# A graph network on one core: the matrix fill split over the engines, and softmax carries applied by masks

## The reference

```python
x = _layernorm(x + _L0_gnn_ref(x, ...), axis=-1)               # attention, 4 heads
x = _layernorm(x + _L1_gnn_ref(x, ...), axis=-1)               # relational
x = _layernorm(x + _L2_gnn_ref(x, edge_weight, src, dst, 3), axis=-1)   # row = src, col = dst
x = _layernorm(x + _L3_gnn_ref(x, edge_index, ...), axis=-1)   # three attention layers, 8 heads

# L2
for _ in range(num_layers):
    msgs = w * X[col]
    X = jax.ops.segment_sum(msgs, row, num_segments=n)
# L0 and L3, per head
m = jax.ops.segment_max(scores, dst, num_segments=N)
e = jnp.exp(scores - m[dst])
denom = jax.ops.segment_sum(e, dst, num_segments=N)
```

## Time and profile before

| | us |
|---|---|
| three runs | 9757.88, 9770.26, 9777.77 |
| median | 9770.26 |
| the profiled execution | 9781.8 |
| its span, first to last instruction | 9780.3 |
| first and last start of the fill's copy on POOL | 3052.9, 4142.0 |
| forward scan of g0 begins, subtraction of g0 begins | 5681.53, 5751.08 |

### The profile page before, as it was taken

One profiled execution on the slowest core, in us unless ns is written; L12 is line 12 of the kernel. 1 busy time (PEld: TensorE's weight loads), 2 busy tenths in 40 slices (PEclk: granted clock), 3 DMA queues, 4 the chain that ended last, 5 costly groups with the idle time before them and its releaser, 6 DMA issues. The chain is left out here.

```text
span 9780.3 us, 183226 instructions
## 1 busy us (share of the span) xinstructions
PE 7267.8 (74%) x30867; PEld 5489.8 (56%) x30868; DVE 6308.2 (64%) x11370; ACT 908.7 (9%) x3742; POOL 4750.5 (49%) x5670
## 2 busy tenths in 40 slices
PE   1899979899997777756666639866663986666388
PEld 1899969788884334313444427644442774444266
DVE  1333356688865777701777867767786776778777
ACT  0222211100010000001000002200000220000012
POOL 0777610477644888800777710077771006777200
PEclk9999999899988999965888969788886987888798
DMA  9444445455531333384777756367775636777564
GB/s 43 113 119 121 118 139 187 118 154 154 151 107 59 108 108 108 114 318 176 187 189 190 196 134 170 105 179 190 192 195 138 169 114 168 188 190 196 143 167 122
DMA packets 1717750, 1476.66 MB, mean 151 GB/s; under 512 B 951333, under 2 KB 1311774, under 8 KB 1717140
## 3 DMA queue, kind: packets, MB, share of 16 engines
q1 hardware_dynamic: 1437876, 949.34, 36.4%
q0 software_dynamic: 163424, 409.43, 16.3%
q10 hardware_dynamic: 116352, 116.73, 3.5%
HBM read 1110.02 MB, written 364.81 MB: 151 GB/s over the span
## 5 line engine op out<-in xcount | busy, mean ns | idle before, releaser
L620 POOL DMA_INDIRECT gx<-table_g,gi x2352 | 2227.4, 947 | 798.9 <-issue 637.0
L859 PE MATMUL ps<-rows,oh 128*128 x5280 | 1722.8, 466 | 1072.6 <-POOLq L597 643.9
L859 PEld LDWEIGHTS ps<-rows,oh 128*128 128x128 f32 x5280 | 1114.3, 227 | 1653.2 <-POOLq L597 844.7
L1196 PE MATMUL ps<-work,oh 128*128 128x273 f32 (+1 forms) x7040 | 1661.2, 405 | 296.7 <-DVE work L1150 261.5
L1196 PEld LDWEIGHTS ps<-work,oh 128*128 128x128 f32 x7040 | 1359.1, 227 | 597.7 <-issue 230.0
L593 POOL COPY gi<-src_i 128x16 int32 (+1 forms) x250 | 51.3, 205 | 2321.9 <-ACTq L694 1670.3
L1150 DVE TENSOR_TENSOR work<-rows,xl 128x1024 f32<-128x1024 f32 (+1 forms) x880 | 872.6, 992 | 471.4 <-PE ps L1196 270.8
L736 DVE TENSOR_TENSOR work<-gx,ps 128x768 f32<-128x768 f32 x660 | 629.8, 954 | 687.3 <-PE ps L861 603.4
L1657 POOL TENSOR_SCALAR oh<-gx,lin 128x196 f32<-128x196 f32 x1176 | 906.2, 785 | 81.7 <-POOL lin L1653 81.2
L1382 PE MATMUL ps<-work,oh 128*128 128x272 f32 x3520 | 862.3, 398 | 45.8 <-issue 31.4
L620 POOL DMA_INDIRECT gx<-table_r,gi x784 | 742.8, 947 | 310.0 <-issue 196.4
(11 more groups left out here) (291 smaller groups left out, 7806.1 us busy)
## 6 DMA issues: line engine op xcount, KB each, us to landing
oh<-hot_d SPq DMA_DIRECT2D x880, 256.0 KB, 2.7
oh<-hotT_d SPq DMA_DIRECT2D x660, 256.0 KB, 3.0
big<-dense_d SPq DMA_DIRECT2D x96, 784.0 KB
dense_d<-big SPq DMA_DIRECT2D x588, 98.0 KB
dense_d<-big ACTq DMA_DIRECT2D x588, 98.0 KB, 1.7
hotT_d<-ohT SPq DMA_DIRECT2D x220, 256.0 KB
hot_d<-oh ACTq DMA_DIRECT2D x220, 256.0 KB, 2.0
ohT<-hotT_d SPq DMA_DIRECT2D x220, 256.0 KB
```

Source lines behind the costliest of these rows:

```text
L620: pool.indirect_dma_start(m.gx[:, u, k, 0:w], None, table, bass.IndirectOffsetOnAxis(m.gi[:, odd, u * K + k:u * K + k + 1].bitcast(U32), 0 ...
L859: ins = nc.tensor.matmul(to, turned, rows, start=True, stop=not adds)
L1196: ins = nc.tensor.matmul(sums(u), m.oh[:, u, k, :], rhs(u % 2)[:, k, :], start=(k == 0), stop=(k == K - 1))
```

## The change

In the fill:

- `places` (0 or 1) and `spots` (times the weight) become two steps. VectorE makes places for two visits in one instruction, with the node numbers read from a PSUM bank, one turn ahead of their use. ScalarE multiplies each by its weight with a Copy activation whose scale is a column of `v_w`.
- POOL makes the high one-hots of visits 0 to 2 of a turn, VectorE that of visit 3 (`last_high`), between its sums.
- `spots`, `his` and `sums` are rings of eight, `places` holds two turns, the PSUM banks remain four; `sums` moves from `m.big` to `m.work`. The loops cover two turns in a pass.
- SP stores visits 0 to 2 and loads their home rows together; ScalarE stores visit 3 two turns late, after the scalings of the turn.
- The filler has 256 columns, not 512. The spill rows are eight, not four.

In the softmax, VectorE makes for each direction, before it waits for the scores, a mask by one scan over the cuts: 0 from a partition's beginning (or end) up to the first cut, -1e30 or less behind it. The backward scans follow the forward scans at once, one carry round serves both directions, and the carry is applied with the mask by an elementwise `max(mask + carry, value)` in place of a second scan.

The diff, cut to its core:

```diff
@@ softmax_parts
+            low = m.work[:, 1, 0:1]
+            step(nc.vector.memset(low, -BIG))
+            for n_way, (way, cuts) in enumerate(zip(ways, (m.new_seg, m.end_seg))):
+                step(nc.vector.tensor_tensor_scan(ends[n_way][:, way], cuts[:, way], low.to_broadcast([P, RUN]),
+                                                  0.0, ALU.add, ALU.max))
+                edge = RUN - 1 if not n_way else 0
+                step(nc.vector.tensor_copy(flags[n_way], ends[n_way][:, edge:edge + 1].to_broadcast([P, heads])))
             dve.wait_ge(s("in"), 16)
...
-                step(nc.vector.tensor_reduce(m.c8[:, 3, 0:1], cuts[:, :], AX.X, ALU.min))
...
                 for h in range(heads):
-                    ins = nc.vector.tensor_tensor_scan(by_head[1][:, h, way], cuts[:, way], by_head[1][:, h, way],
-                                                       carry[:, h:h + 1], ALU.add, ALU.max)
+                    ins = nc.vector.scalar_tensor_tensor(out=by_head[1][:, h, :], in0=ends[n_way],
+                                                         scalar=carries[n_way][:, h:h + 1], in1=by_head[1][:, h, :],
+                                                         op0=ALU.add, op1=ALU.max)
@@ dense_fill, VectorE
+            def place(i, half, c):
+                if not c:
+                    need(dve, s("spots"), (i - 1) * RING)
+                at, wide = c * RING // 2, RING // 2
+                nc.vector.tensor_tensor(
+                    places[:, half, c * wide * P:(c + 1) * wide * P].rearrange("p (n q) -> p n q", n=wide),
+                    node_no.unsqueeze(1).to_broadcast([P, wide, P]),
+                    m.v_key[:, bass.ds(i * RING + at, wide)].unsqueeze(2).to_broadcast([P, wide, P]),
+                    ALU.is_equal).then_inc(s("places"), 1)
+            def last_high(i, odd):
+                nc.vector.tensor_scalar(his[:, odd * RING + last, :], m.hi_no[:, :],
+                                        m.v_hi[:, bass.ds(i * RING + last, 1)], None,
+                                        ALU.is_equal).then_inc(s("last_high"), 1)
-                nc.vector.tensor_scalar(spots[:, u, :], m.iota_row[:, :], m.v_key[:, bass.ds(v, 1)],
-                                        m.v_w[:, bass.ds(v, 1)], ALU.is_equal, ALU.mult).then_inc(s("hot"), 1)
+            def turn(i, odd, more=True):
+                add(i, odd, 0)
+                if more:
+                    place(i + 1, 1 - odd, 0)
+                add(i, odd, 1)
+                if more:
+                    place(i + 1, 1 - odd, 1)
+                add(i, odd, 2)
+                if more:
+                    last_high(i + 1, 1 - odd)
+                add(i, odd, 3)
@@ dense_fill, ScalarE
+            def scale(i, odd):
+                act.wait_ge(s("places"), (i + 1) * 2)
+                act.sem_inc(s("turn_act"), 1)
+                for u in range(RING):
+                    v = i * RING + u
+                    need(act, s("made"), v - 2 * RING + 1)
+                    act.sem_inc(s("spot_act"), 1)
+                    nc.scalar.activation(spots[:, odd * RING + u, :], places[:, odd, u * P:(u + 1) * P], ACT.Copy,
+                                         scale=m.v_w[:, bass.ds(v, 1)]).then_inc(s("spots"), 1)
+            with act.Fori(3, turns - 1, 2) as i:
+                scale(i, 1)
+                store(i - 2, 1)
+                scale(i + 1, 0)
+                store(i - 1, 0)
@@ dense_fill, PE
-                nc.tensor.matmul(m.ps[:, RING + u, :], m.ident_b[:, :], filler, start=True, stop=True)
+                nc.tensor.matmul(m.ps[:, 4 + 2 * (u % 2), 0:2 * P], m.ident_b[:, :], filler, start=True, stop=True)
```

More of the change, by code:

```diff
@@ L1605, in dense_fill, with in_turns @@
 def dense_fill(nc, m):
[L1607 to L1615, removed]
+    places = m.ohT
+    spots = m.work[:, 0, 0:2 * RING * P].rearrange("p (n q) -> p n q", n=2 * RING)
+    his = m.one_hots[:, 0:2 * RING * HIS].rearrange("p (n h) -> p n h", n=2 * RING)
+    sums = m.work[:, 1, 0:2 * RING * HIS].rearrange("p (n h) -> p n h", n=2 * RING)
+    filler = m.iota_b[:, :].unsqueeze(1).to_broadcast([P, K, P])[:, 0:2, :]
+    node_no = m.ps[:, 5, 0:P]
+    stored_rows = m.dense_d.rearrange("(w p) h -> w p h", p=P)
+    turns, last = VISITS // RING, RING - 1
+    def in_turns(eng, turn):
+        for i in range(2):
+            turn(i, i)
+        with eng.Fori(2, turns - 1, 2) as i:
+            turn(i, 0)
+            turn(i + 1, 1)
     with ExitStack() as ctx:
@@ new lines, in _ @@
+            nc.vector.memset(sums[:, 2 * RING - 1, :], 0.0)
+            nc.vector.tensor_copy(node_no, m.iota_row[:, :]).then_inc(s("numbers_set"), 1)
+            dve.wait_ge(s("numbers_set"), 1)
+            for c in range(2):
+                place(0, 0, c)
+            last_high(0, 0)
+            for i in range(2):
+                turn(i, i)
+            with dve.Fori(2, turns - 2, 2) as i:
+                turn(i, 0)
+                turn(i + 1, 1)
+            turn(turns - 2, 0)
+            turn(turns - 1, 1, False)
@@ L1647, in _ @@
             numbers = m.lin[:, 0, 0:RING]
[L1649 to L1658, removed]
@@ L1686, in _, with turn @@
+            for v in range(2 * RING):
+                body(v // RING, v % RING, v // RING)
+            with pe.Fori(2, turns, 2) as i:
+                for odd in range(2):
+                    for u in range(RING):
+                        body(i + odd, u, odd)
         @block.sync
         def _(sp):
-            store(sp, (0, 2))
-        @block.scalar
-        def _(act):
-            store(act, (1, 3))
+            def turn(i, odd):
+                homes = nc.values_load_multi_w_load_instructions(
+                    m.v_home[0:1, bass.ds(i * RING, last)], engines=(mybir.EngineType.SP,),
+                    min_val=0, max_val=NWIN + 2 * RING - 1)[1]
+                for u in range(last):
+                    slot = odd * RING + u
+                    sp.wait_ge(s("summed"), i * RING + u + 1)
+                    sp.sem_inc(s("turn_sp"), 1)
+                    sp.dma_start(stored_rows[bass.ds(homes[u], 1)].rearrange("a p h -> (a p) h"), sums[:, slot, :]
+                                 ).then_inc(s(f"stored{slot}"), 16)
@@ L1695, in dense_layers @@
+            in_turns(sp, turn)
+            for odd in range(2):
+                for u in range(last):
+                    sp.wait_ge(s(f"stored{odd * RING + u}"), 8 * turns)
 def dense_layers(nc, m):
```

122 lines of the change are left out of this document (74 added, 48 removed).

## The result

| | before | after |
|---|---|---|
| runs | 9757.88, 9770.26, 9777.77 | 9870.77, 9873.32, 9876.95 |
| median, us | 9770.26 | 9873.32 |
| span of the profiled execution, us | 9780.3 | 9871.6 |
| turn of the fill, us | 3.717 | 4.096 |

The ratio is 1.0102, with the interval 1.0085 to 1.0119: the change makes the kernel **slower by 1.0%**. The forecast was 9527 us, faster by 2.5%. It was wrong in size and in sign, and its range did not hold the time. The table's turn is taken from GpSimd's copies before and from SyncE's loads after. GpSimd, which runs up to two turns ahead of PE, ends the fill early, so its copies after would give 4.045; SyncE's loads before give 3.72.

A forecast was written before the change was run, and what follows sets the result against it. Pool was taken to bound the fill, with a chain through ScalarE nearly tied, at 2.98 us a turn. From 9781.8 us, minus 216 (fill), 27 (softmax) and 11.5 (profiled run to median), came 9527 us, range 9475 to 9635.

The forecast's parts named there:

- SP's term: In the fill, SP issuing three stores and loading three homes takes 1.5 to 2.6 us a turn.
- Pool at 2.90 to 2.95 us: In the fill, Pool's turn with three one-hots, the copy and two gaps takes 2.90 to 2.95 us.
- VectorE's sizes: In the fill, a double place one-hot takes 0.43 us and `last_high` 0.34; VectorE's turn is about 2.7 us.
- ScalarE's scalings: In the fill, one scaling by weight takes 0.40 us alone, four in a turn 1.2 to 1.8 us.
- The landing has a turn of slack behind the eight slots: In the fill, with eight slots, the landing of stores has one turn to spare.
- The ring at 2.9 to 3.1: In the fill, the chain VectorE places, ScalarE scales, PE multiplies, VectorE adds takes 2.9 to 3.1 us a turn.
- rival (a): In the fill, the VectorE-ScalarE-PE chain or ScalarE sets the turn at about 3.3 us: 9621 us in all; chance 0.18.
- Softmax 27 us: The softmax stages save 27 us (12 to 58) through one carry round and elementwise carry operations.
- the row with a stride: In the softmax, carry operations were priced from a strided reduction, 1.69 us each, against 1.14 without penalty.
- rival (c): In the softmax, the mask operations run at full rate with the fill as forecast: 9496 us in all; chance 0.17.
- Rival (b), PE's clock: In the fill, the halved filler drops PE to 1.2 GHz: 3.47 us a turn, 9671 us in all; chance 0.06.
- Rival (d): In the fill, slow ScalarE scalings make the change lose once a turn exceeds 3.81 us; chance 0.03.

The follow-up runs named there:

- all_four: Kernel after, with five stores per two turns on SyncE and three on ScalarE, no bounds checks, ScalarE's stores one turn earlier, places two turns ahead: 9524.69 us.
- balanced_no_check_early: Kernel after, with five stores per two turns on SyncE and three on ScalarE, no bounds checks on either, ScalarE's stores one turn earlier: 9651.67 us.

## Why the prediction was wrong

**The step that failed is SP's term**, "1.2 + 0.3 to 3 x 0.45, so 1.5 to 2.6 us". SP's turn measured 4.10 us. Three stores are not "0.34 each plus about 0.07": one follows the other by 0.66 to 0.69 us, of which the DMA instruction is 0.33; the wait, the semaphore's step and the address registers are the rest. The load of three homes is 0.95 us and its checks 1.02, not 0.3 to 1.35 together. That leaves about 0.1 us a turn for the loop: 4.10 - (0.69 + 0.66 + 0.66) - 0.95 - 1.02. Even the upper end of my bounds came from adding the instructions that I knew of, and not from a row that shows how long SP takes for one store in all. That row was there: SP's waits of the kernel before, 248.1 of 1080 us, hence 1.43 us a store. Times three it is 4.30 us, over the 3.81 us that I had named as the point where the change loses. I read the waits of PE and GpSimd, and "GpSimd bounds the fill" was right, but I did not ask how far behind the next one was. SP stands in none of the page's busy figures, and I took the absence for room.

Point by point:

- *Pool at 2.90 to 2.95 us*: right; 2.94 where it rules (`all_four`).
- *VectorE's sizes*: right; 0.418 for a double place (0.43), 0.317 for `last_high` (0.34). *ScalarE's scalings*: right; 0.386 alone (0.40), four in 1.28 (1.2 to 1.8).
- *"The landing has a turn of slack behind the eight slots"*: not when the stores are issued late. It was the landing that VectorE waited for, about once a turn (266 waits in 254 turns).
- *The ring at 2.9 to 3.1*: too short. 3.23 us, with the handoff to ScalarE at 0.36 (0.1 to 0.3) and the way from there to the add at 1.46 (1.29). With SP's checks left out (3.08 us by its own stream) but the ring as the change has it, the runs give 3.24 us and 9626 us, close to rival (a) at its 9621. So the forecast would have been 100 us too low even without the fault in SP's term, though its range would have held that time.
- *Softmax 27 us*: right; 25 by the trace. One carry round took 4.65 us (4.8), the 16 carry operations 27.53 us (27.0). One of them takes 1.795 us at the median (1.69), of which the overlap in a row hides some, so about 0.7 us for the stride over the 1.076 of the earlier trace rows. The choice of the row with a stride holds, and rival (c) falls. The Trainium skill (VectorE: DVE Perf Modes, errata section) would have 1.07 us for it; its note on cachelines (SBUF, State Buffer) is what the measurement bears out.
- *Rival (b), PE's clock*: it fell, to 0.84 of full speed in the mean over the fill, but the filler's old length brought it back and gained nothing. The Trainium skill (TensorE: Matmul & The Clock Gate, part 1), by which a falling clock follows lack of activity, agrees: PE had the short filler and idled for SP.
- *Rival (d)*, the only slower one, put the fault on ScalarE at 0.03. Its mechanism is wrong, as ScalarE idles 2.81 us a turn; its point of decision was right, and the engine it should have been held against was SP.
- *The chances*, 0.95 for faster, rested on five terms of which one had no row behind its total. That term alone should have held more than 0.04.

Left open: in `all_four` SP shows no wait either, although its stream should be about (2 x 3.08 - 0.66) / 2 = 2.75 us. Its loads take 0.97 us there, against 0.83, which makes it 2.89, next to GpSimd's 2.93. Why they are longer no run tells. VectorE has no wait for a landing, so SP does not hold it up; that GpSimd alone sets the 2.94 is read from its rows, and no run tests it.

## What to carry to other kernels

Before work is moved to a queue's engine, divide the time that it does not wait by the number of its transfers: this price per transfer (1.43 us here), and not the duration of the DMA instruction (0.34), is near what the next one costs (1.31). An engine that shows no wait at all is the first to suspect as the bound, even if the page does not list its busy time; leave some of its work out and see whether the time falls, for in `all_four` two engines show no wait. The largest wait in the list may only have been handed on. When a bound is taken away, sum the next one as carefully, for here three (SyncE 4.10, ring 3.23, GpSimd 2.94) lay behind one another.

## What the runs showed of the hardware

- A store to a row whose number is loaded at run time took SyncE 1.43 us in all (one home each, with check and its share of the loop), a third one in a turn 1.31, of which the DMA instruction is 0.34. Three homes in one load took 0.95 us at the median; single loads in the kernel before took 0.284 at the median and up to 0.435, 0.35 in the mean, so joining three saved little or nothing.
- A bounds check of such a number took 0.34 us, or 0.30 without the shorter load, although the rows on its instructions show 0.152 and 0.018 us.
- A scalar_tensor_tensor of 880 float elements took 1.796 us when one input and the output had their elements 32 bytes apart (eight heads), 1.778 at 16 bytes (stage t, four heads), and 1.076 when all was contiguous.
- Two stores on ScalarE's queue (1.31 us of issue) hold up the activations behind them on the same engine: in `balanced_no_check_early` the scalings start 0.68 us after the second place, behind one store 0.36 us.
